# A graph attention stage in which GpSimd starts every second block of gathers only after the block before has landed

## The chip, the cores and the metric

One core of a Trainium2 chip runs the whole program. The metric is the device time of one execution in microseconds (us). Three runs of the kernel before took 3563.46, 3567.93 and 3569.03 us; the median is 3567.93 us.

## What is computed

One layer of a graph transformer over 12500 nodes with 256 features and 200000 directed edges: a graph attention network (GAT), a linear attention beside it, and after both a mixture of 8 experts of which each node takes two. The part that the change touches is the message passing of the GAT:

```python
h = (x @ W).reshape(n, H, F)
a_src = jnp.sum(h * att_src[None], axis=-1)
a_dst = jnp.sum(h * att_dst[None], axis=-1)
e = jax.nn.leaky_relu(a_src[src] + a_dst[dst], 0.2)
m = jax.ops.segment_max(e, dst, num_segments=n)
...
ex = jnp.exp(e - m[dst])
denom = jax.ops.segment_sum(ex, dst, num_segments=n)
alpha = ex / (denom[dst] + 1e-16)
msg = h[src] * alpha[..., None]
out = jax.ops.segment_sum(msg, dst, num_segments=n)
```

For each edge the row `h[src]` (256 numbers, with 8 scores behind them) is fetched from memory, weighted, and added to the row of its target. The edges come sorted by target.

## The kernel before

The program runs in stages, with barriers between them. `project` normalises x, computes h and the scores, and stores a table `node_rows` of 12544 rows of 264 float32 (1056 bytes) in HBM. Short stages plan the edge stage; one of them, `plan_pairs`, already issues the gathers of the first EARLY = 3 blocks (L786). `attend_edges` is the edge stage. `finish` and `run_experts` follow.

**Blocks and pairs.** The 200000 edges are cut into SUPERS = 391 blocks of SPAN = 512 edges (G = 4 times 128). The targets are cut into 98 windows of 128 nodes. A block whose edges reach into the next window is worked on once for each window, so there are PAIRS = 488 pairs of a block and a window.

**The ring.** The rows of a block lie in one of RING = 6 slots of the SBUF tensor `rows`. Block q uses slot q mod 6. Each slot has a semaphore `rows_in[j]`; each of the four gathers of a block adds 16 to it when its rows have landed.

**GpSimd** issues the gathers (`gather`, L1123 to L1134). For each block it waits, where a new turn of six blocks begins, for the list of indices (L1127), then for the slot (L1130: `slot_free` at least q - 5), and then issues four indirect DMAs of 128 rows each (L1133). Blocks 3 to 11 are written out, blocks 12 to 383 stand in a loop of 31 turns with 12 blocks a turn (`UNROLL`), the last seven are written out again.

**SyncE** keeps the account (`track`, L1090). For block q in turn it waits until the rows and the targets of q have landed (L1093, L1094), adds one to `arrived` (L1095), waits until VectorE has made the messages of all pairs of the blocks up to q - 2 (L1101), adds one to `slot_free` (L1102), and fetches the targets of block q + 4 (L1084) and now and then a list of indices (L1088). So block q can be gathered when block q - 4 has landed and the pairs of block q - 6 have been weighed.

**The pairs.** VectorE, ScalarE and TensorE run the 488 pairs in straight-line code that `in_pairs` (L1067) writes out, each step with a lag in pairs. For a pair VectorE compares targets with the window (`hotT`, L1189, after waiting for `arrived`), folds the target scores (L1195), adds the sources' scores (L1202), and makes the messages (`msg`, L1213). TensorE turns the one-hot (L1391), multiplies for the target scores (L1401) and sums the messages into the window (L1411, 8 passes); ScalarE copies and takes exponents. Between the pairs lie the 98 tiles of the linear attention: in the first half keys, values and queries (L1423, L1426, L1435), in the second half the outputs (L1445 to L1468).

Of the kernel before, what the change touches and what calls it, by code (L numbers as in the profile page):

```python
# [27 lines left out]
G = 4  # L28
SPAN = G * P
SUPERS = -(-E // SPAN)  # L30
RING = 6
# [918 lines left out]
def attend_edges(nc, s, plan, x, w_out, b_out, out):  # L950


    with ExitStack() as ctx:
# [57 lines left out]
        rows_in = plan.rows_in  # L1011
# [51 lines left out]
        UNROLL = 2 * RING  # L1063
        LOOPS = SUPERS // UNROLL
        KEEP = RING // 3

        def in_pairs(steps, lag, at=()):  # L1067
            for n in range(PAIRS + max(lag)):
                for k, step in enumerate(steps):
                    if 0 <= n - lag[k] < PAIRS:  # L1070
                        step(n - lag[k], (n - lag[k]) % PAIR_RING)
                for table, late, step in at:
                    if n - late in table:
                        step(table[n - late])

        with nc.Block() as block:

            @block.sync
            def _(sp):
                table = s.src_table.rearrange("(p c) o -> p (c o)", p=P)  # L1080

                def fetch_targets(q):
                    j = q % RING
                    sp.dma_start(targets[:, j, :], s.dst_row[q * SPAN:(q + 1) * SPAN, :].rearrange("n o -> (n o)").partition_broadcast(P))\  # L1084
                      .then_inc(targets_in[j], 16)

                def fetch_index(turn):
                    sp.dma_start(index[:, turn % 2, :], table[:, turn * TURN:(turn + 1) * TURN]).then_inc(index_in[turn % 2], 16)  # L1088

                def track(q):  # L1090
                    j = q % RING
                    turn = q // RING
                    sp.wait_ge(rows_in[j], turn * (16 * G) + 16 * G)  # L1093
                    sp.wait_ge(targets_in[j], turn * 16 + 16)  # L1094
                    sp.sem_inc(arrived, 1)  # L1095
                    if q < KEEP:
                        return
                    before = q - (KEEP - 1)
                    weighed = sp.value_load(plan.pairs_before[before // PAIR_RING:before // PAIR_RING + 1, before % PAIR_RING:before % PAIR_RING + 1],
                                            min_val=1, max_val=PAIRS)  # L1100
                    sp.wait_ge(msg_ready, weighed)  # L1101
                    sp.sem_inc(slot_free, 1)  # L1102
                    if q + RING - KEEP < SUPERS:
                        fetch_targets(q + RING - KEEP)
                    if j == RING - 1 and turn + 2 < TURNS:
                        fetch_index(turn + 2)

                fetch_index(1)
                for q in range(RING):
                    fetch_targets(q)  # L1110
                sp.dma_start(wo[:, :, :], w_out.rearrange("(c p) n -> p c n", p=P)).then_inc(weights_in, 16)
                sp.dma_start(bout[:, :], b_out.rearrange("(o n) -> o n", o=1)).then_inc(weights_in, 16)
                for q in range(SUPERS):
                    track(q)

            @block.gpsimd
            def _(g):
                g.memset(blank[:, :, :], 0.0).then_inc(blank_set, 1)
                g.wait_ge(blank_set, 1)
                g.iota(blank[:, :, D:D + 1].bitcast(I32).rearrange("p t o -> p (t o)"), [[0, 1]], base=N,  # L1120
                       channel_multiplier=1).then_inc(blank_set, 1)

                def gather(q, m, two_turns):  # L1123
                    j = m % RING
                    b = m // RING
                    if j == 0 or isinstance(q, int) and q == EARLY:
                        g.wait_ge(index_in[b], two_turns * 16 + 16)  # L1127
                        g.sem_inc(s.wait_seen, 1)
                    if not isinstance(q, int) or q >= RING:
                        g.wait_ge(slot_free, q - (RING - 1))  # L1130
                        g.sem_inc(s.wait_seen, 1)
                    for k in range(G):
                        g.indirect_dma_start(rows[:, j, k, :], None, s.node_rows,  # L1133
                                             bass.IndirectOffsetOnAxis(ap=index[:, b, j * G + k:j * G + k + 1], axis=0)).then_inc(rows_in[j], 16)  # L1134

                for m in range(EARLY, UNROLL):
                    gather(m, m, 0)
                with g.Fori(1, LOOPS) as i:
                    for m in range(UNROLL):
                        gather(i * UNROLL + m, m, i)  # L1140
                for q in range(LOOPS * UNROLL, SUPERS):
                    gather(q, q % UNROLL, q // UNROLL)
# [1099 lines left out]
def program(nc, x, src_table, dst_row, dst_table, dst, W, att_src, att_dst, gat_bias, ln_gamma, ln_beta, w_norm1, w_qkv, w_out, b_out, w_norm2,  # L2242
            gamma, beta, Wr, br, W1, b1, W2, b2, out):
    with ExitStack() as ctx:
# [9 lines left out]
        with stage(nc), ExitStack() as plan_ctx:  # L2254
            plan = Plan()
            plan.node_id = plan_ctx.enter_context(nc.sbuf_tensor("pair_node_id", [P, PAIRS], F32))
            plan.entry = plan_ctx.enter_context(nc.sbuf_tensor("pair_entry", [PAIRS // PAIR_RING, PAIR_RING * ENTRY], I32))
            plan.window = plan_ctx.enter_context(nc.sbuf_tensor("pair_window", [PAIRS // PAIR_RING, PAIR_RING], I32))
            plan.pairs_before = plan_ctx.enter_context(nc.sbuf_tensor("pairs_before", [(SUPERS + 1) // PAIR_RING, PAIR_RING], I32))
            plan.rows = plan_ctx.enter_context(nc.sbuf_tensor("rows", [P, RING, G, ROW], F32))  # L2260
            plan.index = plan_ctx.enter_context(nc.sbuf_tensor("index", [P, 2, TURN], I32))
            plan.rows_in = [nc.alloc_semaphore(name=f"c_rows_in{j}") for j in range(RING)]
            plan.index_in = [nc.alloc_semaphore(name=f"c_index_in{b}") for b in range(2)]
            with ExitStack() as row_ctx:
                plan.count = row_ctx.enter_context(nc.sbuf_tensor("count", [P, 512], F32))
                plan.counts_set = nc.alloc_semaphore(name="b_counts_set")
                plan.entry_row = row_ctx.enter_context(nc.sbuf_tensor("entry_row", [1, PAIRS, ENTRY], I32))
                plan.window_row = row_ctx.enter_context(nc.sbuf_tensor("window_row", [1, PAIRS], I32))
                plan.pairs_before_row = row_ctx.enter_context(nc.sbuf_tensor("pairs_before_row", [1, SUPERS + 1], I32))
                check_inputs(nc, s, plan)  # L2270
                sort_by_window(nc, s, dst_table)
                plan_pairs(nc, s, plan)
                shift_by_target(nc, s, plan)
            attend_edges(nc, s, plan, x, w_out, b_out, out)
# [45 lines left out]
```

## Time and profile before

| | us |
|---|---|
| median of the timed runs | 3567.93 |
| span of the profiled execution (its own time; what lies around the span is not shown) | 4403.2 |
| edge stage in the profiled execution, first to last gather of L1133 | 206.3 to 3079.6 |
| TensorE busy over the span | 3041.5 (69%) |
| VectorE busy over the span | 2365.2 (54%) |
| GpSimd busy over the span | 2160.0 (49%) |

The profiled execution is longer than each of the timed ones by more than 800 us. Its durations of single instructions can be read as they are; its idle times belong to that execution. POOL is GpSimd, DVE VectorE, ACT ScalarE, PE TensorE's matmuls, PEld its weight loads, SP SyncE; a q behind the name means the engine's sequencer or the queue of its DMAs. "Issue" is idle time in which the engine waited for nothing that the profile shows; "remote" means that the profile names no instruction as the one that ended the wait. Ends of matmuls are modelled.

### The profile page before, as it was taken

Reading aid. Unit: us, or ns where it says so; the run is one execution under the profiler, and the core shown is the slowest. Engines: PE = TensorE matmul, PEld = TensorE weight load, DVE = VectorE, ACT = ScalarE, POOL = GpSimd, SP = SyncE. Lnnn points to the kernel's source line nnn. Section 1 sums busy time; section 2 is a strip of 40 time slices with the busy share of each in tenths; the row PEclk is TensorE's granted clock in tenths of the full one; section 3 lists DMA queues with packets and bytes.
Section 4 is the critical chain, followed back from the end, with each engine's and each line's share of the span. In section 5 each row is a group of like instructions: output and inputs, shape, how many; then the busy total and the mean of one; then the engine's idle time right before and its main releaser. Section 6 shows DMA issues by size and latency. Waiting matters only on the chain. (4 is left out here: it accounts for less than half of the span.)

```text
span 4403.2 us, 70224 instructions
## 1 busy us (share of the span) xinstructions
PE 3041.5 (69%) x17326; PEld 2470.3 (56%) x17327; DVE 2365.2 (54%) x6486; ACT 1275.7 (29%) x4257; POOL 2160.0 (49%) x2117
## 2 busy tenths in 40 slices
PE   6566666666676776666666777676323349999998
PEld 5444545545555554455555555555323349999997
DVE  7544444444444444545555555555788865555554
ACT  6422222222222222222222222222455523333332
POOL 3255555555555555444444544444066644444444
PEclk9778777878888887878888888888555559999999
DMA  7544444444444444444444444444455724444443
GB/s 262 173 117 117 111 115 112 119 108 111 109 119 111 115 114 117 121 126 121 128 126 122 133 126 125 126 120 111 127 169 186 238 96 71 72 70 72 70 71 55
DMA packets 384652, 529.69 MB, mean 120 GB/s; under 512 B 64276, under 2 KB 323559, under 8 KB 384218
## 3 DMA queue, kind: packets, MB, share of 16 engines
q0 software_dynamic: 114496, 265.49, 25.5%
q1 hardware_dynamic: 185112, 183.84, 14.8%
q10 hardware_dynamic: 84770, 77.19, 5.5%
q8 instruction: 112, 1.84, 0.2%
q14 instruction: 162, 1.33, 0.1%
HBM read 394.80 MB, written 132.72 MB: 120 GB/s over the span
## 5 line engine op out<-in xcount | busy, mean ns | idle before, releaser
L1133 POOL DMA_INDIRECT rows<-node_rows,index x1552 | 1480.9, 954 | 1392.6 <-SPq L1102 930.3
L1411 PE MATMUL ps_sum<-msg,hot 128*128 128x260 f32 x3904 | 1220.7, 465 | 40.0 <-issue 27.9
L1411 PEld LDWEIGHTS ps_sum<-msg,hot 128*128 128x128 f32 x3904 | 853.5, 230 | 198.4 <-issue 45.3
L1391 PE MATMUL ps_hot<-ident_h,hotT 128*128 128x128 bf16 x1952 | 223.5, 247 | 729.7 <-ACT hot L1293 338.6
L1391 PEld LDWEIGHTS ps_hot<-ident_h,hotT 128*128 128x128 bf16 x1952 | 154.3, 110 | 832.8 <-issue 549.4
L1213 DVE TENSOR_TENSOR msg<-rows,ps_w 128x1024 f32<-128x1024 f32 x488 | 596.1, 1222 | 45.1 <-ACT ps_w L1305 29.1
L2140 POOL DMA_INDIRECT out_dram<-big x204 | 352.7, 1729 | 438.3 <-DVE big L2232 390.9
L1195 DVE TENSOR_REDUCE e<-ps_tgt 128x32 f32<-128x96 f32 x488 | 123.3, 253 | 801.2 <-remote 728.2
L1293 ACT ACTIVATE hot<-ps_hot 128x512 f32<-128x512 bf16 x488 | 290.2, 595 | 736.3 <-remote 589.0
L2166 PEld LDWEIGHTS x_ps_hT<-x_rowsT,x_w_now 128*128 128x128 f32 x3264 | 398.0, 192 | 11.5 <-DVE x_w_now L2210 1.1
L2166 PE MATMUL x_ps_hT<-x_rowsT,x_w_now 128*128 128x128 f32 x3264 | 399.1, 276 | 0.7 <-DVE x_w_now L2210 0.7
L2175 PE MATMUL x_ps_out<-big,x_actT 128*128 x1632 | 386.0, 379 | 0.4 <-ACT x_actT L2191 0.4
L2191 ACT ACTIVATE x_actT<-x_ps_hT,b1T 128x128 f32<-128x128 f32 x816 | 233.3, 369 | 522.9 <-issue 382.9
L1700 POOL DMA_INDIRECT expert_in<-f_rows,f_slot x196 | 261.2, 1333 | 232.1 <-ACT f_rows L1743 175.2
L2175 PEld LDWEIGHTS x_ps_out<-big,x_actT 128*128 128x128 f32 x1632 | 294.2, 190 | 32.3 <-issue 0.7
L1298 ACT ACTIVATE e<-e 128x16 f32<-128x16 f32 x488 | 106.9, 219 | 636.7 <-DVE e L1207 400.4
L1279 DVE TENSOR_TENSOR area<-ps_kv,area 128x256 f32<-128x256 f32 x98 | 41.6, 425 | 454.0 <-remote 285.2
L2205 DVE COPY x_rowsT<-x_ps_t 128x256 f32<-128x256 f32 x204 | 86.7, 425 | 243.1 <-PE x_ps_t L2156 231.8
L1230 DVE TENSOR_TENSOR big<-big,ps_sum 128x260 f32 x488 | 204.5, 419 | 17.6 <-issue 8.7
L1189 DVE TENSOR_SCALAR hotT<-targets,pair_node_id 128x512 bf16 x488 | 174.9, 359 | 67.8 <-SPq L1095 38.2
L1318 ACT ACTIVATE area<-ps_kv 128x256 f32<-128x256 f32 x98 | 37.6, 383 | 589.3 <-remote 376.1
L1423 PE MATMUL ps_kv<-wq,area 128*128 128x512 f32 x392 | 196.8, 626 | 4.1 <-DVE area L1239 2.0
(289 smaller groups left out, 4194.9 us busy)
## 6 DMA issues: line engine op xcount, KB each, us to landing
targets<-dst_row SPq DMA_DIRECT2D x391, 128.0 KB
big<-expert_in SPq DMA_DIRECT2D x204, 130.0 KB
rows<-node_rows,index POOLq DMA_INDIRECT x1564
node_rows<-big SPq DMA_DIRECT2D x14, 924.0 KB
turned<-rT SPq DMA_DIRECT2D x14, 896.0 KB, 4.6
area<-turned ACTq DMA_DIRECT2D x98, 128.0 KB
queries<-area ACTq DMA_DIRECT2D x98, 128.0 KB
area<-queries ACTq DMA_DIRECT2D x98, 128.0 KB
```

What stands on the lines that cost most here:

```text
L1133: g.indirect_dma_start(rows[:, j, k, :], None, s.node_rows, bass.IndirectOffsetOnAxis(ap=index[:, b, j * G + k:j * G + k + 1], axis=0)).th ...
L1213: v.tensor_tensor(m[:, :, 0:D].rearrange("p g (h f) -> p g h f", h=GH), rows[:, bass.ds(here, 1), :, 0:D].rearrange("p j g (h f) -> p (j g ...
L1230: v.tensor_tensor(dest, dest, ps_sum[:, j % 2, 0:SUM], ALU.add).then_inc(sum_added, 1)
L1293: act.activation(hot[:, j % MSGS, :], ps_hot[:, 0:SPAN], ACT.Copy).then_inc(hot_ready, 1)
L1391: mm = pe.transpose(ps_hot[:, k * P:(k + 1) * P], hotT[:, j % 2, k * P:(k + 1) * P], ident_h[:, :])
L1411: mm = pe.matmul(ps_sum[:, j % 2, 0:SUM], hot[:, j % MSGS, k * P:(k + 1) * P], msg[:, j % MSGS, k, :], start=(k == 0), stop=(k == G - 1))
L1423: pe.matmul(ps_kv[:, :], rT[:, u, c * P:(c + 1) * P], s.wq[:, c, D:3 * D], start=(c == 0), stop=(c == C - 1))
L1700: g.indirect_dma_start(s.expert_in, bass.IndirectOffsetOnAxis(ap=slot[0:count, j, k, i:i + 1], axis=0), rows[0:count, j, i, :], None).then ...
L2140: g.indirect_dma_start(out, bass.IndirectOffsetOnAxis(ap=rows[:, j, D:D + 1].bitcast(I32), axis=0), outs[:, j, :], None, compute_op=ALU.ad ...
L2166: mm = pe.matmul(ps_hT[:, j % 2, k * P:(k + 1) * P], w1_now[:, j % 2, a:a + P], rowsT[:, j % 2, c, :], start=(c == 0), stop=(c == C - 1))
L2175: mm = pe.matmul(ps_out[:, j % 2, 0:D], actT[:, j % 2, c, :], s.w2[:, bass.ds(e, 1), c * D:(c + 1) * D].rearrange("p e n -> p (e n)"), sta ...
L2191: ins = act.activation(actT[:, j % 2, c, :], ps_hT[:, j % 2, c * P:(c + 1) * P], ACT.Gelu, bias=s.b1T[:, bass.ds(e * HC + c, 1)])
```

## The change

For every block with an even place m in its turn of twelve (that is, every even q from 4 on), GpSimd waits, after the wait for the slot and before its four gathers, until the semaphore of the slot before shows that all four gathers of block q - 1 have landed. The gathers themselves, their order and all other engines' instructions stay.

```diff
         KEEP = RING // 3
+        PACE = 2
+        LANDED = 16 * G
...
                     if not isinstance(q, int) or q >= RING:
                         g.wait_ge(slot_free, q - (RING - 1))
+                        g.sem_inc(s.wait_seen, 1)
+                    if m % PACE == 0:
+                        last = (m - 1) % RING
+                        g.wait_ge(rows_in[last], two_turns * (32 * G) + (m - 1) // RING * (16 * G) + LANDED)
                         g.sem_inc(s.wait_seen, 1)
                     for k in range(G):
                         g.indirect_dma_start(rows[:, j, k, :], None, s.node_rows,
```

The lines below L1063 move down by two, those below L1130 by six: the gathers of L1133 stand at L1139 afterwards.

GpSimd's instructions at the start of its loop over the blocks, before. A row is one instruction or a run of equal ones, with the semaphores that it waits for; the numbers of semaphores are used again from stage to stage, and this list prints the name that a number had first: `a_w_in` is the list of indices here.

```order
L1138 ISA
L1130 ISA [waits a_w_in]
L1133 DMA rows<-node_rows,index 128x264 [waits c_slot_free]
L1133 DMA rows<-node_rows,index 128x264 x3
L1130 REGISTER_ALU
L1133 DMA rows<-node_rows,index 128x264 [waits c_slot_free]
L1133 DMA rows<-node_rows,index 128x264 x3
L1130 REGISTER_ALU
```

The same place after. `a_last_loaded` is `rows_in[5]` here and `a_x_loaded0` is `rows_in[1]`.

```order
L1144 ISA
L1132 ISA [waits a_w_in]
L1136 REGISTER_ALU [waits c_slot_free]
L1139 DMA rows<-node_rows,index 128x264 [waits a_last_loaded]
L1139 DMA rows<-node_rows,index 128x264 x3
L1132 REGISTER_ALU
L1139 DMA rows<-node_rows,index 128x264 [waits c_slot_free]
L1139 DMA rows<-node_rows,index 128x264 x3
L1132 REGISTER_ALU
L1136 REGISTER_ALU [waits c_slot_free]
L1139 DMA rows<-node_rows,index 128x264 [waits a_x_loaded0]
```

What moved: nothing changes places. The first gather of each even block has a wait for the rows of the slot before it, one register step computes the count to wait for, and the wait for the slot stands one instruction earlier.

## Rows read from the trace of the kernel before

**Rows 1.** The page's head and busy times: engine, us (share) x instructions.
```profile
span 4403.2 us, 70224 instructions
PE 3041.5 (69%) x17326; PEld 2470.3 (56%) x17327; DVE 2365.2 (54%) x6486; ACT 1275.7 (29%) x4257; POOL 2160.0 (49%) x2117
```
**Rows 2.** Stretches: us, busy us (count) PE, PEld, DVE, ACT, POOL; PEclk, DMA share, GB/s.
```profile
206.30:3079.60 2873.30, 1963.18 (x10534) 1480.28 (x10534) 1393.80 (x3684) 686.28 (x2512) 1480.86 (x1552) 0.82 0.44 119
3650.00:4350.00 700.00, 700.00 (x4882) 661.36 (x4881) 379.80 (x1126) 214.01 (x748) 323.99 (x188) 1.00 0.45 71
3100.00:3600.00 500.00, 170.84 (x790) 158.60 (x788) 409.68 (x1070) 229.04 (x475) 263.31 (x218) 0.51 0.54 174
0.00:206.30 206.30, 125.23 (x593) 95.19 (x594) 129.61 (x464) 118.22 (x424) 61.20 (x142) 0.88 0.66 223
```
**Rows 3.** Line L1133: busy us, mean ns, idle before, by releaser; durations.
```profile
L1133 POOL DMA_INDIRECT rows<-node_rows,index x1552 | 1480.9, 954 | 1392.6 <-SPq L1102 930.3 <-issue 462.3
L1133 POOL DMA_INDIRECT rows<-node_rows,index x1552: 943/949/1192, 206.3 to 3078.7; - x194
  SPq L1102: 930.3, 192
  issue: 462.3, 1360
```
**Rows 4.** Waits in the edge stage: us in total, times, longest.
```profile
DVE e L1195 <- remote: 723.5, 116, 12.5
```
**Rows 5.** DVE and PE, 1002.8 to 1016 us: start, us, instruction, [idle before].
```profile
1015.90 0.26 DVE L1195 TENSOR_REDUCE e<-ps_tgt 128x32 f32<-128x96 f32 x1 [10.34 <-remote]
...
1002.57 0.40 PE L1391 MATMUL ps_hot<-ident_h,hotT 128*128 128x128 bf16 x4 [0.47 <-DVE hotT L1189]
1002.82 0.26 PE L1401 MATMUL ps_tgt<-reach_parts,hotT 128*128 x4
1003.15 1.99 PE L1411 MATMUL ps_sum<-msg,hot 128*128 128x260 f32 x8
...
1007.14 0.94 PE L1426 MATMUL ps_q<-area,wq 128*128 128x128 f32 x7
```
**Rows 6.** GpSimd's gathers without a break; a block begins at 1024.08.
```profile
1022.83 0.95 POOL L1133 DMA_INDIRECT rows<-node_rows,index  x1 [0.30 <-issue]
1024.08 0.95 POOL L1133 DMA_INDIRECT rows<-node_rows,index  x1 [0.30 <-issue]
```
**Rows 7.** A slot's release and the gather that waited for it.
```profile
1018.29 0.34 SPq L1084 DMA_DIRECT2D targets<-dst_row  x1
1019.02 0.99 POOL L1133 DMA_INDIRECT rows<-node_rows,index  x1 [5.46 <-SPq L1102]
```
**Rows 8.** DMA share and GB/s (last two columns) behind two last gathers; the probes' landing.
```profile
1032.85:1033.85 1.00, 0.00 (x0) 0.00 (x0) 0.00 (x0) 0.00 (x0) 0.95 (x1) 0.50 0.47 123
...
1034.85:1035.35 0.50, 0.00 (x0) 0.00 (x0) 0.00 (x0) 0.50 (x3) 0.00 (x0) 0.50 0.28 110
1035.35:1035.85 0.50, 0.00 (x0) 0.00 (x0) 0.00 (x0) 0.50 (x2) 0.00 (x0) 0.50 0.00 0
...
3081.17:3081.67 0.50, 0.00 (x0) 0.00 (x0) 0.28 (x2) 0.38 (x1) 0.00 (x0) 0.50 0.44 76
...
DMA to landing us min/median/max: 2.5/5.0/9.3
```
**Rows 9.** Messages of two pairs in turn, rows at hand.
```profile
1016.97 1.22 DVE L1213 TENSOR_TENSOR msg<-rows,ps_w 128x1024 f32<-128x1024 f32 x1
1020.03 1.22 DVE L1213 TENSOR_TENSOR msg<-rows,ps_w 128x1024 f32<-128x1024 f32 x1
```
**Rows 10.** TensorE at the lower granted clock, 1036.8 to 1043.8 us.
```profile
1036.84 0.59 PE L1391 MATMUL ps_hot<-ident_h,hotT 128*128 128x128 bf16 x4 [7.94 <-ACT hot L1293]
1037.22 0.31 PE L1401 MATMUL ps_tgt<-reach_parts,hotT 128*128 x4
1037.38 3.80 PE L1411 MATMUL ps_sum<-msg,hot 128*128 128x260 f32 x8
1040.98 2.85 PE L1423 MATMUL ps_kv<-wq,area 128*128 128x512 f32 x4
```

## The prediction

> **What bounds the kernel now.** I read the page's head and the busy times by stretch first, because the profiled execution is far longer than the timed ones. Its span is 4403.2 us [rows 1], and what lies around the span is not shown (taken as nothing); the median of the three runs is 3567.93 us, 835 us less. So the first question is which stretch of the trace is longer than in a timed run, and every sum below has to say in which of the two it stands.
>
> The table of stretches answers it [rows 2]. From the first gather of the edge stage to the last (206.3 to 3079.6 us) lie 2873.3 us. After it, the experts' stretch shows PE busy for 700 of 700 us at clock 1.00, so nothing there can be shorter; between them DVE is busy for 410 of 500 us, and in the first 206 us for 130. In the edge stretch no engine is near its full time: PE 1963, POOL 1481, DVE 1394 of 2873 us. The waits say why [rows 4]: DVE stood 116 times, 723.5 us, before the small reduction of L1195 for a release that the trace names nowhere. One such hole is in [rows 5]: DVE idles for 10.34 us up to 1015.90 us, although the matmuls of L1401 that the reduction reads stand at 1002.82 us. Some 720 us in holes of this kind account for most of the 835 us, so I take them to be absent, or small, in the timed runs. I place all of the 835 us in the edge stretch: outside it lie 4403.2 - 2873.3 = 1529.9 us, so the timed stretch has 3567.9 - 1529.9 = 2038 us, or 5.25 us for each of the 388 blocks gathered in it.
>
> What fills those 2038 us is read from GpSimd's own line [rows 3]. It issues 1552 gathers, 4 for a block. Being busy takes 1480.9 us, and the idle time before them that waited for nothing ("issue") 462.3 us: together 1943 us, 1.25 us a gather, as the starts in [rows 6] also show. The remaining 930.3 us of the profiled stretch is waiting for SyncE's count of free slots (L1102). In the timed stretch only 2038 - 1943 = 95 us are left for that. So in the timed runs GpSimd issues gathers nearly without a break: **the serial issue on GpSimd bounds the edge stage**, at 5.01 us a block against 5.25 us. The other engines keep up: where the rows are there, messages follow each other every 3.05 us a pair [rows 9], and a block has 488/391 = 1.25 pairs, 3.8 us of work in 5.25 us.
>
> **The change, part by part.**
> Added instructions: for every second block one wait, one count of a semaphore and, in the loop, one register addition. They are the sequencer's, which runs ahead: the 0.30 us between two gathers are the same where a block ends and the slot wait stands between them (before 1024.08 us) as inside a block [rows 6]. Cost nothing as long as a gather of 0.95 us runs meanwhile; if that cover is gone they stand in the resume time below, which is measured with such steps in it.
>
> The wait itself: blocks 4, 6, ..., 390, that is 194 of them, start only when the four gathers of the block before have landed. Queued behind the waiting instruction are this block's four gathers and those of the next block; SyncE's tracking, and behind it DVE's one-hot, wait for these. Nothing on SP, ACT, DVE or PE is moved.
>
> What one wait costs: before, the first gather of the even block starts 1.25 us after the last gather of the odd one. Now it starts L + R after it: L is the time from that start to the landing, R the time from the semaphore to the start of a gather that was held.
> R: SyncE's next transfer starts at 1018.29 us right behind its release of a slot, and the held gather starts at 1019.02 us [rows 7], so R is 0.73 us.
> L has no row of its own, so I bound it by traffic [rows 8]. The last gather before a pause starts at 1032.85 us; DMA moves 110 GB/s in the half microsecond up to 1035.35 us and nothing after: L is at most 2.5 us there. Behind the stage's last gather at 3078.67 us traffic runs, with other engines' transfers among it, to 3081.67 us: at most 3.0 us. Far off, the 18 probes of the first stage, gathers of 128 single words with over 200 GB/s of other traffic beside them, took 2.5, 5.0 and 9.3 us (minimum, median, maximum). I take 2.6 us, near the row of the same instruction in the same stage, a little up for the blocks whose neighbours' transfers share the engines.
> So a wait adds 2.6 + 0.73 - 1.25 = 2.08 us, 194 of them 404 us; with L 2.5 it is 384 us, with 3.0 481 us, with 5.0 869 us. It cannot add less than zero, since no gather becomes cheaper by it.
>
> The Trainium skill, in "DMA: Bandwidth & Descriptors", section "Anatomy of one DMA — SWDGE (gpsimd) path", gives a fixed 2.0 us and the bytes at 436 GB/s: my estimate for 128 rows of 1056 bytes is 2.3 us. By that figure a wait adds 1.78 us and the sum 345 us, for 3818 us; the trace agrees within 0.2 us.
>
> What is hidden: the 95 us that the timed stretch may hold beside GpSimd's own 1943 us. With GpSimd 2 us slower every two blocks, the six slots are released earlier than they are asked for, so I let these 95 us go. Then the stretch is 1943 + 404 = 2347 us, and the time 1529.9 + 2347 = **3877 us**, 309 us or 8.7% more. Of the 462.3 us of "issue" some 47 us (462.3 less 1360 times 0.305) are longer pauses, about one at each turn of the loop, whose first block is an even one: up to 47 us may vanish into the new waits.
>
> In the profiled execution the same change should cost less than 404 us, because there GpSimd stood 930.3 us anyway, 192 times, 4.8 us each: such a wait before an even block ends after the rows before it have landed, and the new wait adds nothing to it.
>
> **The rivals.**
> 1. GpSimd is not the bound in the timed runs, because a gather costs less there than under the profiler. The point of decision: two blocks take 10.5 us now; after the change 7 steps between gathers plus 2.6 + 0.73 us. These are equal when a step is 1.02 us in place of 1.25 us. Below that the pairs' chain sets the 2038 us before and after: 3568 us, no change, and if the paced gathers also let the other transfers through earlier, some of the 95 us may go, down to 3473 us. For it: the profiled execution is visibly disturbed. Against it: GpSimd's steps are the steadiest rows of the trace (943 ns least, 949 median [rows 3]), and 1943 us explain 95% of the timed stretch without any fitting. The pairs' chain would have to be slow by itself, against 3.8 us a block.
> By the Trainium skill, same page, section "Queues, rings and completion order", each DMA engine goes round its queues packet by packet, so queued gathers cannot hold other queues off; by that rule the relief, and with it the 3473 us, falls away. A DMA share of 0.44 in the stretch [rows 2] agrees.
> 2. The wait does not bite, because GpSimd arrives late at an even block, held by the slots, when the rows have landed. In the profiled execution the slots hold it 192 times, 4.8 us each. In the timed stretch 95 us leave room for some 20 such waits, so 174 waits would bite: 362 us and the 95 us stay, 3930 us. It only decides if most waits are free, which needs hundreds of microseconds of slot waits that the timed runs have no room for.
> 3. PE becomes the bound: its gaps grow, and its granted clock falls. At 1.0 (2.4 GHz) a pair takes 0.40 + 0.26 + 1.99 us [rows 5], at 0.5 (1.2 GHz; so granted at 1035 us [rows 8]) 0.59 + 0.31 + 3.80 us [rows 10]. All 488 pairs at 0.5 are 2294 us, just under 2347 us; with the 98 key and query tiles, 2.85 us for the first four matmuls [rows 10] and about twice the 0.94 us of [rows 5] for the rest, 4.7 us each, they are 2755 us: 4285 us. For it: the clock was 0.82 over the stretch [rows 2]. Against it: it came back to 1.0 whenever PE had work behind it, as in the experts' 700 us, and a PE that falls behind has just that.
>
> **How the numbers follow.** Forecast as worked out, GpSimd's serial chain with the landing exposed (rival 2's partial form included): 0.84, 3877 us, by itself 3780 to 3990 us. Rival 1: 0.10, of which 0.06 within 0.2% and 0.04 faster. Rival 3 or a mixture with it: 0.06. The range: below, if a gather step is 0.1 us shorter in timed runs, the stretch is 388 x 4 x 1.15 + 194 x 2.18 = 2208 us, 3738 us; if instead half of the 166 us in which the busiest engine idles in the first and the finishing stretch were also profiling, 3794 us. Above, if the 95 us stay, 3972 us, and with L 3.0 as well, 4049 us. I take 3730 to 4020 us, which leaves out rivals 1 and 3 (0.16) and some 0.04 of the main case. 0.2%, about 7 us, is what a measurement can tell from no change here: faster 0.04, same 0.06, slower 0.90.
>
> **What would show it.** In the profile after, GpSimd's gather line must have about 190 waits whose releaser is the DMA of the rows, the idle time before such a gather between 1.9 and 2.5 us where GpSimd was not held by slots; waits for SyncE's slots must shrink by hundreds of microseconds; the busy time of the 1552 gathers must stay at 1480 us. The time must grow by about 2 us per even block. A time within 20 us of 3568 us would say that GpSimd had slack in the timed runs; a growth beyond 450 us that landing takes 3 us or more, or that PE has become the bound; then PE's clock in the stretch would be well under 0.82.

## The result: 4061 us, slower by 13.9%, and more than forecast

The changed kernel took 4061.13 us (median of four runs, 4057.28 to 4063.24). The kernel before, run beside it, took 3568.48 us. The ratio is 1.1387, with a 95% interval of 1.1367 to 1.1406. The forecast had the sign right, but it added 309 us where 493 us came, and 4061 us lies above its range.

The head of the profile after answers to [rows 1]. This execution's span agrees with the timed runs.

```profile
span 4061.6 us, 70511 instructions
```

The stretches after answer to [rows 2]; the columns are the same.

```profile
0.00:209.70 209.70, 125.52 (x592) 95.54 (x593) 129.93 (x466) 118.45 (x424) 62.13 (x141) 0.87 0.64 220
209.70:2750.70 2541.00, 1938.82 (x10613) 1443.47 (x10614) 1398.00 (x3711) 694.97 (x2534) 1473.21 (x1552) 0.88 0.51 134
...
3300.00:4000.00 700.00, 700.00 (x4876) 661.21 (x4875) 379.59 (x1126) 215.03 (x752) 327.32 (x188) 1.00 0.45 71
```

The edge stretch takes 2541 us, and 4061.6 - 2541.0 = 1520.6 us lie outside it. The line of the gathers answers to [rows 3]: durations, then the idle time of GpSimd before them by releaser (us, times).

```profile
L1139 POOL DMA_INDIRECT rows<-node_rows,index x1552: 940/946/1332, 209.7 to 2749.8; - x194
...
  DMA rows<-node_rows,index: 654.2, 194
  issue: 410.8, 1348
  SPq L1104: 2.7, 9
```

All 194 new waits appear, each with 654.2 / 194 = 3.37 us of idle time. Busy time, issue, waits for rows and waits for slots add up to 1473.2 + 410.8 + 654.2 + 2.7 = 2540.9 us, the whole stretch: GpSimd's chain has no other hole.

Of [rows 4], the small reduction's waits for an unnamed release, nothing is left; VectorE waits for SyncE's count of landed blocks instead (us, times, longest); in the undisturbed execution of the kernel before, shown below, the same wait comes to 342.1 us in 184 times.

```profile
DVE hotT L1195 <- SPq L1097: 816.3, 257, 7.4
```

Two of the new waits, from GpSimd's timeline (start, us, instruction, idle before). They answer to the even steps of [rows 6].

```profile
1256.44 0.94 POOL L1139 DMA_INDIRECT rows<-node_rows,index  x1 [0.30 <-issue]
1259.99 0.95 POOL L1139 DMA_INDIRECT rows<-node_rows,index  x1 [2.60 <-DMA rows<-node_rows,index]
...
1492.42 0.94 POOL L1139 DMA_INDIRECT rows<-node_rows,index  x1 [0.30 <-issue]
1496.90 0.94 POOL L1139 DMA_INDIRECT rows<-node_rows,index  x1 [3.54 <-DMA rows<-node_rows,index]
```

From the last gather of a block to the first of the next it is 3.55 us in the first case and 4.48 us in the second, where 3.33 us had been forecast. During the second pause the queues of ScalarE and SyncE issue transfers of their own, 0.7 us after the start of the last gather:

```profile
1493.08 0.35 ACTq L1317 DMA_DIRECT2D area<-turned  x1
1493.13 0.33 SPq L1086 DMA_DIRECT2D targets<-dst_row  x1
```

In the first pause the same two are issued 1.4 us after that start (at 1257.87 and 1257.92 us).

### The profile page after: what moved, and what is told of

Its sections match the earlier page's. It is cut to its first block and busy times, and to the rows that moved or that the text cites. A ratio compares the mean times of both kernels' runs of the same rounds, so it can differ in the third digit from the quotient of the medians.

```text
span 4061.6 us, 70511 instructions
## 1 busy us (share of the span) xinstructions
PE 3006.7 (74%) x17326; PEld 2424.5 (60%) x17327; DVE 2357.5 (58%) x6486; ACT 1278.3 (31%) x4257; POOL 2156.4 (53%) x2117
## 5 line engine op out<-in xcount | busy, mean ns | idle before, releaser
L1139 POOL DMA_INDIRECT rows<-node_rows,index x1552 | 1473.3, 949 | 1067.8 <-DMA rows<-node_rows,index 654.2
L1417 PE MATMUL ps_sum<-msg,hot 128*128 128x260 f32 x3904 | 1176.9, 454 | 20.0 <-DVE big L1236 4.2
L1417 PEld LDWEIGHTS ps_sum<-msg,hot 128*128 128x128 f32 x3904 | 828.1, 223 | 173.3 <-issue 8.9
L1195 DVE TENSOR_SCALAR hotT<-targets,pair_node_id 128x512 bf16 x488 | 188.3, 386 | 819.7 <-SPq L1097 816.3
L1397 PE MATMUL ps_hot<-ident_h,hotT 128*128 128x128 bf16 x1952 | 207.8, 234 | 565.3 <-DVE hotT L1195 562.2
L1397 PEld LDWEIGHTS ps_hot<-ident_h,hotT 128*128 128x128 bf16 x1952 | 132.1, 103 | 677.7 <-DVE hotT L1195 667.8
L2238 DVE SCALAR_TENSOR_TENSOR big<-x_ps_out,x_weight,x_bias 128x256 f32<-128x256 f32 x204 | 98.7, 484 | 122.1 <-issue 116.2
```

The costliest lines, as they stand in the source:

```text
L1139: g.indirect_dma_start(rows[:, j, k, :], None, s.node_rows, bass.IndirectOffsetOnAxis(ap=index[:, b, j * G + k:j * G + k + 1], axis=0)).th ...
L1397: mm = pe.transpose(ps_hot[:, k * P:(k + 1) * P], hotT[:, j % 2, k * P:(k + 1) * P], ident_h[:, :])
L1417: mm = pe.matmul(ps_sum[:, j % 2, 0:SUM], hot[:, j % MSGS, k * P:(k + 1) * P], msg[:, j % MSGS, k, :], start=(k == 0), stop=(k == G - 1))
```

## What the experiments asked

Theory A, the prediction's: GpSimd's serial issue bounds the edge stage, and each wait lays one landing open on that chain. Its rivals: GpSimd is not the bound; the loss comes from holding gathers back at all; the wait is longer than forecast because of a fixed latency, or because of other traffic.

**The kernel before, profiled once more.** The 835 us between the profiled execution and the timed runs had to be placed by argument.

> The kernel before, unchanged, profiled once more. If the 835 us between its profiled span and its timed runs belong to the one profiled execution, this profile's span is 3560 to 3620 us, GpSimd waits 60 to 130 us for slots, and no reduction of the edge scores waits for an unnamed release. If they belong to the profiling of this kernel, the span is again over 4300 us with over 700 us of such waits. Its gathers then show what a gather costs where the span agrees with the timed runs: I expect 0.95 us busy and 0.30 us of gap either way.

It took 3573.91 us. The head of its page:

```profile
span 3572.2 us, 70224 instructions
```

Its edge stretch, with the columns of [rows 2] (the row begins 3 us before the first gather and ends 2 us before the last one is done; from one to the other it is 2046.5 us):

```profile
206.00:2253.50 2047.50, 1740.45 (x10560) 1315.97 (x10561) 1387.76 (x3700) 690.63 (x2521) 1479.07 (x1552) 0.96 0.63 167
```

Its gathers: busy us, mean ns and idle time before, then durations, then GpSimd's idle time by releaser (us, times):

```profile
L1133 POOL DMA_INDIRECT rows<-node_rows,index x1552 | 1480.7, 954 | 565.9 <-issue 451.4
...
L1133 POOL DMA_INDIRECT rows<-node_rows,index x1552: 942/949/1427, 209.1 to 2254.6; - x194
...
  issue: 451.4, 1436
  SPq L1102: 114.5, 116
```

The 835 us belonged to that one execution, whose holes [rows 4, 5] are gone here. The stretch is 2047 us (forecast 2038), its slot waits 114.5 us (forecast 95); most of these stand late, 87 us of them after 1500 us. From these lines to those of the kernel after, the gathers' busy time changes by -7, issue by -41, slot waits by -112 and waits for rows by +654 us: +494 us in sum, against 493 us between the timed medians. So the whole loss stands on GpSimd's line.

**Is GpSimd the bound?** One memset of 128x1024 follows each odd block's gathers, 194 of them, without any wait for rows (each waits for the memset two blocks earlier, which is done by then):

```diff
+                    if m % 2 == 1:
+                        ...
+                        g.memset(pad[:, :], 0.0).then_inc(pad_set, 1)
```

> The kernel before, with one added memset of 128x1024 on GpSimd behind the gathers of every odd block (194 in all, about 0.9 us each by the 0.32 us of the 128x260 memset in the trace; with the gap behind it 1.0 to 1.2 us). Theory A, GpSimd's serial issue bounds the edge stage in the timed runs: 194 to 233 us more, less at most the 95 to 100 us in which GpSimd still waits for slots: 3670 to 3800 us. Theory B, the pairs' chain bounds the stage and GpSimd has slack: 3560 to 3580 us.

3677.15 us beside 3566.81 us: ratio 1.0309 (1.0292 to 1.0327), 110 us more. The memsets' group on its page (busy us, mean ns, idle before):

```profile
L1142 POOL MEMSET pad<- 128x1024 f32 x194 | 188.1, 970 | 0.1
```

GpSimd's idle time before the gathers there (us, times):

```profile
  issue: 412.1, 1365
  SPq L1104: 62.8, 74
  POOL pad L1142: 18.6, 113
```

Of 188 us of memsets, with 19 us of gaps behind them, 110 us reach the end. The rest took the place of idle time: slot waits fell from 114.5 to 62.8 us, issue from 451 to 412 us. A rival in which GpSimd has slack of 1 us for each two blocks would have shown no change, so GpSimd is the bound wherever it does not wait for a slot.

The same memsets in the changed kernel, in front of its new wait:

> The changed kernel with the same 194 memsets at the same place, which is now the pause in which GpSimd waits for the landing (mean idle 3.37 us in the profile after). Theory A, the pause is the latency from the last gather to its landing and its length is set by the DMA: the memset is hidden, 4050 to 4075 us. Rival, the pause is set by GpSimd itself (the wait and the restart of its queue cost that much wherever they stand): 4230 to 4300 us.

4054.0 us, ratio 1.136 (1.1338 to 1.1382): within 8 us of the change alone. The waits for rows shrink by what the memsets take: 467.6 us of waits and 188.1 us of memsets are 655.7 us, and the change alone waits 654.2 us. The memsets' group on the page, and then the wait in the line of the gathers:

```profile
L1148 POOL MEMSET pad<- 128x1024 f32 x194 | 188.1, 970 | 0.0
```

```profile
  DMA rows<-node_rows,index: 467.6, 194
```

So the end of a pause is set by the landing, whatever GpSimd does meanwhile.

**Holding back, or an exposed landing?** In this version the wait is for the first two gathers of the block before alone (they have a semaphore of their own, and SyncE waits for both), so two further gathers, 2.5 us, lie between the last one waited for and the wait:

```diff
-                        g.wait_ge(rows_in[last], two_turns * (32 * G) + (m - 1) // RING * (16 * G) + LANDED)
+                        g.wait_ge(half_in[last], two_turns * (32 * H) + (m - 1) // RING * (16 * H) + LANDED)
```

> The changed kernel, but the wait asks only for the first two of the four gathers of the block before (they count on a semaphore of their own; SyncE waits for both). Theory A, what is paid is the latency behind the gather waited for: two steps of 1.25 us of it are now hidden behind gathers three and four, so the idle time falls from 3.37 to about 0.9 us, 0.56 us above a normal gap, 194 times 108 us above GpSimd's own issue: 3575 to 3680 us. Rival, holding gathers back costs by itself (pauses in the stream, rows that arrive in lumps): the loss stays for the most part, 3800 us and more.

3594.59 us, ratio 1.0081 (1.0064 to 1.0098). Idle time before its gathers (us, times):

```profile
  issue: 458.9, 1425
  DMA rows<-node_rows,index: 76.3, 59
  SPq L1107: 65.3, 68
```

3594.59 us are 28 us more than the 3566.81 us of the kernel before beside it, where the change costs 493 us. The 194 waits, counts and register steps are all still there, and only 59 waits are seen, 1.3 us each. So what costs the time is neither the instructions nor the order, but the part of a landing that no other gather covers.

**How the loss grows with the number of waits.** `PACE = 4` gives 97 waits, `PACE = 1` a wait at every block, 387.

> The changed kernel with the wait before every fourth block in place of every second (97 waits). Theory A, each wait costs the same 3.07 us on GpSimd's chain: 298 us above GpSimd's own issue, 3764 us, up to 3860 us with the slot waits that the kernel before has. Rival, the loss comes from something that is not proportional to the waits (PE's clock, the ring running dry): near 4060 us or near 3570 us.

> The changed kernel with the wait before every block in place of every second one (387 or so waits). Theory A (each wait exposes one landing on GpSimd's serial chain, 3.07 us above the normal gap): the stretch is 1946 + 387 x 3.07 = 3134 us, with 1520 us outside 4650 us; if landings quicken because less is in flight, 4550 us. Rival B (part of the loss comes from something else that the change disturbs, such as the order of slots, and does not grow with the number of waits): well under 4400 us. Every fourth block gave 3758 us, so by proportion 0.5 : 1 : 2 the steps are about 190, 493 and 985 us, less the slot waits that each pause absorbs once.

Every fourth block: 3758.14 us, ratio 1.0541 (1.0524 to 1.0559). Every block: 4539.91 us, ratio 1.2721 (1.2699 to 1.2742). The idle time before the gathers by releaser (us, times), every fourth block:

```profile
  DMA rows<-node_rows,index: 315.2, 97
  SPq L1104: 11.9, 39
```

The same with a wait at every block:

```profile
  DMA rows<-node_rows,index: 1170.3, 387
  issue: 374.8, 1152
  SPq L1104: 3.7, 12
```

The steps over the kernel before are 191, 493 and 970 us for 97, 194 and 387 waits; one wait is 3.25, 3.37 and 3.02 us long. Less the 0.30 us that the gap has anyway, and less the slot waits that each version swallows, this makes 97 x 2.95 - 103 = 184, 194 x 3.07 - 112 = 484 and 387 x 2.72 - 111 = 943 us, within 30 us of each measurement. At every block a wait is 0.35 us shorter than at every second, at a DMA share of 0.44 in place of 0.51 over the stretch, so the expected 4650 us were too many, and the 4550 us that were expected for quicker landings came close.

**Why 3.37 us and not the 2.38 us that the forecast's figures give?** (3.33 us from start to start, less 0.95 us of the gather.) First, other loads of the stage are left out, those of the targets in this way and most of those of the attention's tiles likewise; the results are then computed from stale data, and only the time is of use:

```diff
+                    if q >= RING:
+                        sp.sem_inc(targets_in[j], 16)
+                        return
```

> The changed kernel, with most of the other loads of the edge stage left out: the transfers of the targets after the first six, and the loads of the attention's tiles (rT, query and x rows) after the first two of each; semaphore counts stand in their place, so the results are computed from stale data. Theory A (a wait costs more than forecast because the last gather lands later when other queues' transfers share the DMA engines: 2.4 us alone, up to 3.7 us beside 256 KB of others): the wait shrinks from 3.37 us to 2.7 to 2.9 us, 194 of them give back 90 to 130 us, time 3930 to 3970 us. Rival B (the 3.37 us are the fixed latency of a landing and of the restart): the wait stays within 0.15 us, time 4030 to 4060 us.

3946.92 us, ratio 1.106 (1.1042 to 1.1079), 114 us less than the change. A wait is 544.2 / 194 = 2.81 us; 0.57 us less, 194 times, is 110 us. Idle time before its gathers:

```profile
  DMA rows<-node_rows,index: 544.2, 194
  issue: 410.6, 1348
```

Second, the gathers themselves are made small (`W` is 32 from the seventh block on):

```diff
-                        g.indirect_dma_start(rows[:, j, k, :], None, s.node_rows,
+                        g.indirect_dma_start(rows[:, j, k, 0:W], None, s.node_rows,
```

> The changed kernel with 32 in place of 264 numbers of each row gathered from the seventh block on (128 bytes in place of 1056 for each of the 128 rows; the messages are computed from stale data). Theory A (the landing is lengthened by bytes, its own and others'): a landing takes 0.5 to 0.9 us less, the wait 2.5 to 2.9 us, time 3880 to 3960 us. Rival B (a fixed latency per gather and restart): the wait stays within 0.15 us of 3.37, time 4030 to 4060 us. GpSimd's busy time of a gather stays at 0.95 us in both, since it is the issue of 128 descriptors.

3998.41 us, ratio 1.1214 (1.1195 to 1.1234), 63 us less than the change, short of theory A's 3880 to 3960 us and outside rival B's range too. The waits in its line of the gathers:

```profile
  DMA rows<-node_rows,index: 589.8, 194
```

Two stretches of it, early and late, with the columns of [rows 2]; the gathers are POOL's count:

```profile
400.00:900.00 500.00, 367.31 (x1897) 272.99 (x1898) 241.97 (x635) 126.58 (x472) 290.29 (x304) 0.85 0.27 50
...
1900.00:2400.00 500.00, 410.98 (x2452) 308.82 (x2452) 338.64 (x927) 156.05 (x554) 307.61 (x326) 0.93 0.35 85
```

Although seven eighths of the rows' bytes are gone, a wait shrinks by 0.33 us on average, from 3.37 to 3.04 us. It is uneven: GpSimd issues 304 gathers in the early 500 us, the same number as the change does there with whole rows, and 326 in the late, where the change issues 310. In the early part an average last gather has 217 KB of other queues' transfers beside it, 146 KB in the change; in the late part 158 KB, 185 KB in the change. So the early part has more of other traffic in each pause, which may be why it gains nothing; that was not tried by itself. What a landing takes is in any case not mainly the movement of the rows' own bytes.

The trace records every packet of a gather and the semaphore's update, so each pause can be cut into three parts. No view prints them; they are worked out for all pauses of a kernel (the last gather's start, the end of its last packet, the update that releases GpSimd, the next gather's start), means in us:

| kernel | start to last packet | to the update | to the next start | sum |
|---|---|---|---|---|
| forecast | 2.6 | no term | 0.73 | 3.33 |
| change | 3.17 | 0.37 | 0.78 | 4.32 |
| fewer other loads | 2.60 | 0.37 | 0.78 | 3.75 |
| every block | 2.84 | 0.36 | 0.78 | 3.97 |
| narrow rows | 2.78 | 0.44 | 0.77 | 4.00 |

The first part goes with what the other two queues move in that time. In the changed kernel it is 2.44 us in the 21 pauses with none of it, 3.09 us with 64 to 128 KB, 3.68 us in the 50 with more than 256 KB. A longer landing also has more time to count bytes in, so it is the version with fewer other loads that shows the cause: 3.17 us become 2.60 us. These bytes are not all that counts. With a wait at every block 203 KB of them move beside an average last gather, against 181 KB in the change, and it still takes 2.84 us; fewer of GpSimd's own gathers are under way there, but whether that is the reason was not tried. In the undisturbed execution of the kernel before, without any pause, the last gather of an odd block takes 3.55 us from its start to the last update of its semaphore (mean of the 116 odd blocks whose updates the trace has in full), against 3.17 + 0.37 = 3.54 us in the pauses of the change: the landings did not become longer by the change, they were that long.

The Trainium skill, in "DMA: Bandwidth & Descriptors", section "Latency and other measured facts", puts most of a transfer's fixed cost down to the memory's latency and says that a lighter load on HBM makes that cost smaller. The trace agrees as far as it goes: 2.60 us where other loads are left out, 3.17 us where they run. Whether HBM or the engines that the queues share is the place was not tried.

## Why the prediction was right in sign and short in size

- **The timed stretch.** Placing the 835 us in the edge stretch was right: 2038 us were taken, 2047 us are read from the second execution of the kernel before. The rest, 1529.9 us in the forecast, is 1526 us in that execution and 1521 us after the change.
- **GpSimd's serial issue as the bound.** Right: 1943 us of its own work were taken, 1932 us measured, and added work on GpSimd reaches the end. (The two messages of [rows 9] start 3.06 us apart, not 3.05; nothing hangs on it.) Rival 1, a gather that is cheaper in timed runs, fell: the median gather is 949 ns in both executions of the kernel before, and the second one's span agrees with the timed runs.
- **That the wait bites.** Right, and more fully than needed: 194 of 194. Rival 2 did not come about.
- **The 95 us of slot waits vanish.** Right: 114.5 us become 2.7 us. The longer pauses at the turns of the loop went as well: "issue" fell by 41 us, while the forecast allowed up to 47 us and took none.
- **The price of one wait: this step failed.** 2.6 + 0.73 - 1.25 = 2.08 us were taken, 4.32 - 1.25 = 3.07 us came. 0.99 us, 194 times, are 192 us; the miss is 493 - 309 = 184 us. Of the 0.99 us, 0.57 us are L, which was read behind a gather beside which no other queue moved anything [rows 8], in an execution whose holes had left the queues empty. In the changed kernel 181 KB of other transfers move while an average last gather is under way. That the value taken, 2.60 us, is also the mean of the kernel with fewer other loads is chance. The bound of 3.0 us was misread: in the half microsecond behind the row of [rows 8] the trace still has traffic (the last column is GB/s),

```profile
3081.67:3082.17 0.50, 0.14 (x2) 0.17 (x3) 0.50 (x2) 0.40 (x3) 0.00 (x0) 0.50 0.06 17
```

so that gather took 3.4 us to its last packet. The prediction took other engines' transfers to be among this traffic; all packets of that time are GpSimd's own. This gather fetches only the filler behind the last edge, 128 times the same row, so it is no measure of the others. The probes' median of 5.0 us, beside other traffic and dismissed as far off, was a warning. Another 0.37 us lie between the last packet and the semaphore's update: L was read to the end of the traffic, and R from the release on, so this piece stood in neither term. R itself was right to 0.05 us.
- **Rival 3, PE as the bound.** It is busy for 1939 of 2541 us at a clock of 0.88, above the 0.82 of [rows 2], and with a wait at every block for 2117 of 3027 us at 0.81. It idles more the longer the gathers take, and GpSimd's own line accounts for the whole stretch, so it follows the gathers and does not hold them.
- **What was to show it.** About 190 waits by the DMA of the rows, unchanged busy time and vanished slot waits came as said; the idle time of 1.9 to 2.5 us did not (3.37 us). A growth above 450 us was to mean a landing of 3 us or more, or PE as the bound: it is the first.
- **The profiled execution** was to lose less than 404 us; its span fell by 342 us instead, since it lost its holes. That says nothing on the change.

No version tried here is faster than the kernel before. Of the 2047 us of its edge stage 1932 us are the gathers and the gaps between them, and 114.5 us are slot waits.

## What to carry to other kernels

Where one engine issues transfers serially and its issue time alone fills the stage, as here, a wait of that engine for the transfer that it has just issued puts the latency behind it on the end, once per wait, less the gap and the other waits that it takes in: count the waits, and measure from the start of the last transfer to the start of the next instruction, as one duration, rather than adding pieces from different places of the trace. Read a latency from a stretch with the traffic that the timed run has; the profiled execution that was 835 us longer than the timed runs had emptier queues and flattered it. If a pace is wanted, wait for a transfer that was issued a latency earlier: two gathers further back, 2.5 us, took 493 us down to 28 us.

## What was not expected of the hardware

- One profiled execution of the kernel before was 835 us longer than its timed runs, with over 700 us of waits that the trace names nowhere. The next one, and those of all the changed kernels, agree with their timed runs within 0.3%. The first trace also holds only half as many updates of semaphores as the second (35258 against 68675), so that a wait for a release "that the trace names nowhere" can be one whose record is missing. A span that disagrees with the timed runs is worth a second execution before anything is read from it.
- With the same matmuls, TensorE is busy 1740 us in the kernel before and 1939 us after, at a mean granted clock of 0.96 and 0.88 over the stretch, in which it stands idle for 15% and 24%; with a wait at every block it is 0.81 and 30%. No run here changes the idle time alone, so that the idle time brings the clock down is not shown. The time it costs TensorE was hidden behind GpSimd.
